# A one-layer decoder on one core: ten lower parts of the expert weights by VectorE, and another pace of splitting them

## The reference

```
x = layernorm(x + mixer(x))                 # state-space mixer, 4 sequences of 512
x = layernorm(x + xattn(x, ctx_1024))       # 16 heads of width 8, 256 keys
x = layernorm(x + ffn(x))                   # mixture of experts

def ffn(inputs):                            # E = 8 experts, top 2, D = 128, F = 512
    weights, selected = top_k(inputs @ gate_kernel, 2)
    weights = softmax(weights)
    # rows sorted by expert, each row once for each of its two experts
    hidden = silu(rows @ w0[e]) * (rows @ w1[e])
    rows_out = hidden @ wo[e]
    return weighted_sum_over_the_two(weights, rows_out)
```

## Time and profile before

| what | value |
|---|---|
| median of 3 runs | 422.5 us |
| the runs | 418.44, 422.5 and 1061.15 us |
| the profiled execution | 415.8 us |
| its span, first to last instruction | 414.5 us |
| granted TensorE clock, mean | 0.98 |
| busy: TensorE, VectorE, ScalarE, GpSimd | 349.5, 292.3, 235.2, 230.4 us |
| first and last product with a split weight on TensorE | start at 267.8 and 393.4 us |

### The profile page before, as it was taken

The page is one execution under the profiler, slowest core; times in us unless marked ns, Lnnn a source line. Parts: engine busy times, 40 slices in busy tenths (PEclk is TensorE's granted clock), DMA queues, the critical chain, the costliest instruction groups (busy, mean ns, idle before and its releaser), DMA issues.

```text
span 414.5 us, 9020 instructions
## 1 busy us (share of the span) xinstructions
PE 349.5 (84%) x2869; PEld 238.0 (57%) x2869; DVE 292.3 (71%) x836; ACT 235.2 (57%) x460; POOL 230.4 (56%) x341
## 2 busy tenths in 40 slices
PE   1999977888988999988878899988997999999900
PEld 1666645556544545444444445567776899898800
DVE  3555645888788888878796736376776877877737
ACT  2677644432667666455577687744644665666514
POOL 2660598855354435271569788546575445445525
PEclk9999999999999999999999999999999999999975
DMA  8933322636515040322624343211112211111054
GB/s 269 336 110 106 87 85 77 187 94 186 171 33 166 5 140 5 99 70 75 196 69 131 117 155 102 74 32 40 53 41 78 78 53 40 53 52 35 32 171 146
DMA packets 44461, 41.97 MB, mean 101 GB/s; under 512 B 4560, under 2 KB 38416, under 8 KB 44416
## 3 DMA queue, kind: packets, MB, share of 16 engines
q1 hardware_dynamic: 41136, 35.10, 28.1%
q0 software_dynamic: 2272, 4.69, 3.2%
q10 hardware_dynamic: 1008, 1.61, 1.1%
HBM read 26.36 MB, written 14.75 MB: 99 GB/s over the span
## 4 chain that ended last, share of the span: by engine, by line
PE 56%; DVE 20%; issue 7%; POOL 7%; ACT 4%; another core or an unknown queue 3%; DMA 2%; ACTq 0%; DVEq 0%; POOLq 0%
PE banks L1017 12%; DVE nm L1210 8%; PE banks L1044 6%; PE banks L1032 4%; PE banks L859 4%; PE banks L698 4%; PE banks L907 3%; PE banks L1045 2%; PE banks L755 2%; PE banks L937 2%; PE banks L763 2%; DVE ctx_in L1152 2%; PE banks L806 2%; PE banks L934 1%
## 5 line engine op out<-in xcount | busy, mean ns | idle before, releaser
L1210 DVE TENSOR_REDUCE nm<-banks 128x4 f32<-128x1024 f32 x64 | 78.1, 1220 | 17.5 <-PE banks L850 11.4
L1520 ACT ACTIVATE probs_all<-banks 128x1024 f32<-128x1024 f32 x64 | 65.4, 1023 | 36.0 <-PE banks L859 29.6
L1017 PE MATMUL banks<-w_split,scores_in 128*128 x234 | 64.5, 410 | 0.0
L1342 DVE TENSOR_TENSOR ctx_in<-ctx_in,banks 128x512 f32<-128x512 f32 x39 | 26.8, 687 | 27.3 <-ACT ctx_in L1567 21.4
L1017 PEld LDWEIGHTS banks<-w_split,scores_in 128*128 128x128 f32 x234 | 40.8, 189 | 7.7 <-issue 0.9
L1705 POOL DMA_INDIRECT slots_dram<-rows,place_u x32 | 31.9, 996 | 23.5 <-DVE count L1302 16.1
L1727 POOL DMA_INDIRECT y_dram<-x,scatter_u x39 | 38.5, 987 | 11.4 <-POOL x L1723 9.7
L1567 ACT ACTIVATE ctx_in<-banks 128x512 f32<-128x512 f32 x39 | 23.3, 599 | 36.7 <-PE banks L1017 31.9
L859 PE MATMUL banks<-scores_in 32*128 32x256 f32 x256 | 32.2, 326 | 12.0 <-ACT probs_all L1520 6.0
L1044 PE MATMUL banks<-w_split,scores_in 128*128 x156 | 39.1, 327 | 2.8 <-ACT scores_in L1573 2.1
L907 PE MATMUL banks<-probs_all,vals 128*9 128x256 f32 x512 | 39.7, 381 | 0.2
(11 more groups left out here) (230 smaller groups left out, 802.2 us busy)
## 6 DMA issues: line engine op xcount, KB each, us to landing
scores_in<-k_dram SPq DMA_DIRECT2D x32, 128.0 KB, 2.7
scores_in<-q_dram SPq DMA_DIRECT2D x32, 128.0 KB, 2.7
ctx_in<-in_L_ffn_w SPq DMA_DIRECT2D x16, 256.0 KB, 2.7
cs_wide<-cs_dram SPq DMA_DIRECT2D x14, 256.0 KB, 3.7
scores_in<-slots_dram SPq DMA_DIRECT2D x39, 65.0 KB, 1.9
k_dram<-split_qk SPq DMA_DIRECT2D x8, 256.0 KB, 2.5
q_dram<-split_qk SPq DMA_DIRECT2D x8, 256.0 KB, 2.3
ctx_in<-in_L_ffn_wo SPq DMA_DIRECT2D x8, 256.0 KB, 2.9
```

The source lines that it names most:

```text
L1017: m = TE.matmul(up_bank(i, j), xT[:, i % XT, xh, :], all_weights[:, c + j * FF:][:, bass.ds(expert_at[i], FF)], start=n == 0, stop=n == 2)
L1210: V.tensor_reduce(most, maxima_of(n).rearrange("p (j k q) -> p j k q", j=2, k=TPS), AX_X, ALU.max, negate=True).then_inc(s["nmax"], 1)
L1520: C.activation(probs(n).rearrange("p j k q -> p (j k q)"), EXPS, ACT.Exp, scale=SCALE).then_inc(s["probs"], 1)
```

## The change

Ten of the 24 subtractions, those of pieces 14 to 23, go from GpSimd to VectorE, with a semaphore of their own, w_lo_v. Pieces 0 to 3 are loaded at step 34 and the first is split at step 36; no piece is split at steps 40, 41 and 49. So pieces 0 to 3 are split at steps 36 to 39, 4 to 10 at steps 42 to 48, and 11 to 23 at steps 50 to 62, VectorE's ten at steps 53 to 62. The step of piece n loads piece n + 3 in place of n + 2. VectorE's subtraction stands in its queue where split_weights stands in the common list, and waits for ScalarE's copy of the same piece. SyncE's later loads and the first product of the experts wait for both semaphores. In turn_mixed a wait of GpSimd for its own instruction uses the common semaphore of that kind; the instructions are the same.

```diff
@@ -57,6 +57,7 @@
 W_HEAD, W_REST, W_OUT, W_ALL = 0, 2 * FF, 4 * FF, 6 * FF
 W_RING = NT * D // FF
 PIECES = 3 * NE
+POOL_PIECES = 14
 XG, AHEAD = 8, 4
 LAST_ADDED = SLOT_TILES - 3
 XT, TURNED_AHEAD, DOWN_LAG, HS = 3, 2, 3, 3
@@ -206,6 +207,7 @@
 CLEAR_FROM = 23
 TURNED_ALONE = max(END_HALVES) // 2 | 1
 LAST_MIXER = tile_step(NT - 1) + LAGS[0][1]
+WEIGHTS_FROM, WEIGHTS_OMITTED = LAST_MIXER + 2, (40, 41, 49)
 
 
 def front_order():
@@ -288,13 +290,13 @@
                 yield "evacuate", weighed // GR, 0
         yield from (stage for stage in after_attention(n) if stage[0] not in READY)
         yield from mixer_step(n)
-        if n == LAST_MIXER + 4:
+        if n == WEIGHTS_FROM:
             for i in range(W_RING):
                 yield "load_weights", i
-        elif n >= LAST_MIXER + 6 and piece < PIECES:
+        elif n >= WEIGHTS_FROM + 2 and n not in WEIGHTS_OMITTED and piece < PIECES:
             yield "split_weights", piece
-            if W_RING <= piece + 2 < PIECES:
-                yield "load_weights", piece + 2
+            if W_RING <= piece + 3 < PIECES:
+                yield "load_weights", piece + 3
             piece += 1
         yield from tiles_step(n)
         if UNREAD_FROM <= n < 4 and n != 2 or n >= ALL_MAXIMA - 1:
...
@@ -552,6 +554,15 @@
 
             return a["ctx_g0" if g == END_LAST else f"rows{g}"]
 
+        def split_parts(n):
+
+            e, i = divmod(n, 3)
+            raw = w_raw[:, n % W_RING, :]
+            if i < 2:
+                return raw, *(w_split[:, e, c + i * FF:c + (i + 1) * FF] for c in (W_HEAD, W_REST))
+            parts = w_split[:, e, W_OUT:].rearrange("p (c h d) -> p c h d", c=FC, h=2)
+            return raw.rearrange("p (c d) -> p c d", c=FC), parts[:, :, 0, :], parts[:, :, 1, :]
+
         def all_scattered(q):
             for r in range(Y_RING):
                 q.wait_ge(a[f"y_out{r}"], 16 * len(range(r, SLOT_TILES, Y_RING)))
@@ -653,7 +664,8 @@
                 q.wait_ge(s["q_mm"], B)
                 q.wait_ge(a["qw0"], 32 * B // 2)
                 q.wait_ge(a["qw1"], 32 * B // 2)
-                q.wait_ge(s["w_lo"], n - W_RING + 1)
+                q.wait_ge(s["w_lo"], min(n - W_RING + 1, POOL_PIECES))
+                q.wait_ge(s["w_lo_v"], n - W_RING + 1 - POOL_PIECES)
                 if i < 2:
                     SY.dma_start(w_raw[:, r, :], A[f"L0_ffn_w{i}"][e]).then_inc(a[f"e{r}"], 16)
                 else:
...
@@ -1009,7 +1021,8 @@
                 q.wait_ge(s["xT_hi"], i + 1)
                 q.wait_ge(s["xT_lo"], i + 1)
                 q.wait_ge(s["hid"], i - 1)
-                q.wait_ge(s["w_lo"], PIECES)
+                q.wait_ge(s["w_lo"], POOL_PIECES)
+                q.wait_ge(s["w_lo_v"], PIECES - POOL_PIECES)
                 if i == 1:
                     q.wait_ge(s["probs"], NPAIR)
                 for n, (xh, c) in enumerate(((0, W_HEAD), (0, W_REST), (1, W_HEAD))):
...
@@ -1301,6 +1314,13 @@
                 own.settle()
                 V.tensor_tensor(count[:, :], count[:, :], total, ALU.add).then_inc(s["counted"], 1)
 
+            def split_weights(n):
+                if n < POOL_PIECES:
+                    return
+                raw, head, rest = split_parts(n)
+                q.wait_ge(s["w_hi"], n + 1)
+                V.tensor_tensor(rest, raw, head.bitcast(F32), ALU.subtract).then_inc(s["w_lo_v"], 1)
+
             def count_tiles(part):
                 q.wait_ge(s["counted"], PART_BATCHES[part])
                 if part == LAST_PART:
...
@@ -1542,13 +1562,7 @@
                              ACT.Identity).then_inc(s["rows_x2"], 1)
 
             def split_weights(n):
-                e, i = divmod(n, 3)
-                raw = w_raw[:, n % W_RING, :]
-                if i < 2:
-                    head = w_split[:, e, W_HEAD + i * FF:W_HEAD + (i + 1) * FF]
-                else:
-                    raw = raw.rearrange("p (c d) -> p c d", c=FC)
-                    head = w_split[:, e, W_OUT:].rearrange("p (c h d) -> p c h d", c=FC, h=2)[:, :, 0, :]
+                raw, head, _ = split_parts(n)
                 q.wait_ge(a[f"e{n % W_RING}"], 16 * (n // W_RING + 1))
                 C.activation(head, raw, ACT.Identity).then_inc(s["w_hi"], 1)
 
...
@@ -1654,8 +1668,8 @@
             def turn_mixed(b):
                 bb = b % 2
                 q.wait_ge(s["sq"], TPS * (b + 1))
-                G.tensor_scalar(ss[:, bb, :], ss[:, bb, :], 1.0, DI * 1e-6, ALU.mult, ALU.add).then_inc(s["rms_in"], 1)
-                q.wait_ge(s["rms_in"], b + 1)
+                own.step(G.tensor_scalar(ss[:, bb, :], ss[:, bb, :], 1.0, DI * 1e-6, ALU.mult, ALU.add))
+                own.settle()
                 q.wait_ge(s["r1"], TPS * (b - 1))
                 G.tensor_tensor(rms[:, bb, :], ss[:, bb, :], minus_half[:, 0:TPS], ALU.pow).then_inc(s["rms"], 1)
 
...
@@ -1706,13 +1720,9 @@
                                          rows[:, b % 2, i // TPS, i % TPS, :], None).then_inc(a[f"slots{b % 2}"], 16)
 
             def split_weights(n):
-                e, i = divmod(n, 3)
-                raw = w_raw[:, n % W_RING, :]
-                if i < 2:
-                    head, rest = (w_split[:, e, c + i * FF:c + (i + 1) * FF] for c in (W_HEAD, W_REST))
-                else:
-                    raw = raw.rearrange("p (c d) -> p c d", c=FC)
-                    head, rest = (w_split[:, e, W_OUT:].rearrange("p (c h d) -> p c h d", c=FC, h=2)[:, :, h, :] for h in range(2))
+                if n >= POOL_PIECES:
+                    return
+                raw, head, rest = split_parts(n)
                 q.wait_ge(s["w_hi"], n + 1)
                 G.tensor_tensor(rest, raw, head.bitcast(F32), ALU.subtract).then_inc(s["w_lo"], 1)
```

More of the change, by code:

```diff
@@ L324 @@
     "bc_t bcT score_mm score diff fall xdt skip xdec decay mat state_mm state off_mm "
-    "y_mm y_sum y_gated sq yT_t yT rms_in rms out_mm r1 ln1_var ln1_in ln1 x1 x1_t x1T "
+    "y_mm y_sum y_gated sq yT_t yT rms out_mm r1 ln1_var ln1_in ln1 x1 x1_t x1T "
     "q_mm max_mm nmax nm_split nm_t nm_out exp_mm probs av_mm av_lo av_hi heads_t o_norm o_t oT wo_mm "
-    "r2 ln2_var ln2_in ln2 x2 x2_t x2T rows_x2 gate_mm logit ge topped chosen rank_mm counted w_hi w_lo "
+    "r2 ln2_var ln2_in ln2 x2 x2_t x2T rows_x2 gate_mm logit ge topped chosen rank_mm counted w_hi w_lo w_lo_v "
     "xg_t xT_hi xT_lo up_mm sil hid turn_mm hsT_hi hsT_lo down_mm y_half y_add y_x2 y_last "
@@ L1378, in vector_program @@
                           divide=divide, out_project=out_project, x2_norm=x2_norm, gate_top=gate_top, choose=choose,
-                          rank_chosen=rank_chosen, count_tiles=count_tiles,
+                          rank_chosen=rank_chosen, split_weights=split_weights, count_tiles=count_tiles,
                           rank_tiles=rank_tiles, place_tiles=place_tiles,
```

## The result

| | kernel before | changed kernel |
|---|---|---|
| median of 20 executions | 419.72 us | 422.50 us |
| lowest | 416.44 us | 420.73 us |
| profiled execution | 415.8 us | 422.87 us |
| its span | 414.5 us | 421.5 us |
| granted TensorE clock, mean | 0.98 | 0.966 |

The ratio is 1.0073, 95% interval 1.0053 to 1.0092: about 3 us slower. It leaves out executions more than 1.5% above the fastest of the same kernel, which of the changed kernel are 6 of 20, at 429 to 432 us with a mean clock of 0.93 to 0.946. The profiled execution of the kernel before, at 415.8 us, is faster than all of the twenty that were timed, so the two traces lie 7 us apart and the medians 2.8.

What follows compares the result with a forecast made beforehand. Bound: the chain through all engines up to step 50, TensorE's own queue from step 52. Terms +0.5 + 0 + 0 + 0.8 = +1.3 us on 418.4 gave 419.7, rounded to 420; range 414 to 426 us.

Steps and rivals of the forecast that it cites:

- part 2: Steps 40, 41 and 49 without a split: claimed 0, range 0 to -1.0 us; maxima's split 2.5 us earlier.
- The starting point: Base of the sum: the lower undisturbed run, 418.4 us, chosen over the stated median of 422.5 us.
- The copy at step 37: ScalarE's new copy at step 37, where there is no gap, delays exponential 38 on the chain: +0.5 us.
- No split at 40, 41 and 49: Exponentials 42 and 50 start 0.52 us earlier, but 43 and 51 wait for the fourth indirect write: 0.
- The rule read from a few rows: A batch's first steps can't go on before its fourth indirect write ends; TensorE's signals arrive 0.75 to 0.8 us after.
- Loads further ahead: Loads one piece earlier: ScalarE's 0.42 us landing wait goes, the value-bank copy holds exponential 46; 0, range 0 to -0.3.
- The subtraction on VectorE: Ten subtractions at steps 53 to 62: 0.68 us each, range 0.68 to 1.54; only their place costs.
- The late count: Step 57: tile count waits behind VectorE's subtraction, ends at 255.5, delaying the placing of tiles: +0.8 us.
- Rival B: Tile count's whole 2.7 us delay reaches TensorE, or subtractions take 1.54 us: +3.2 us, 421.6 us; chance 0.15.
- The rule that the two engines exclude each other: Two-input VectorE work and GpSimd's SBUF reads block each other; from step 53 VectorE loses blockers, GpSimd's roots gain some.
- Rival D: TensorE stands still 1.5 us at 254, clock falls, expert stage loses tens of us: over 440 us; chance 0.02.

Runs made afterwards that it cites:

- Run 6: The changed kernel with no split at step 37 and one at step 40; ratio 1.0013 to the kernel before.
- run 7: The changed kernel, split at 40 not 37, choices summed by one-input reduction, tile count ahead of its step's subtraction; ratio 1.0008 to the kernel before.
- run 11: Changed kernel, split at 40 not 37, one-input reduction, count ahead of subtraction, indirect writes spread over four steps; ratio 0.9893 to kernel before, median 415.89 us.
- run 9: The kernel before with the four indirect writes of batches 0 to 4 spread, one in each of four steps; ratio 1.0007 to the kernel before.
- run 8: The kernel before with ten subtractions on VectorE and the tile count ahead of its step's subtraction, old pace; ratio 0.9984 to the kernel before.
- run 12: The changed kernel, split at 40 not 37, one-input reduction, tile count still behind the subtraction; ratio 1.0004 to the kernel before, median 426.74 us.
- run 1: The changed kernel with all 24 subtractions on GpSimd, so the new pace alone; ratio 1.0040 to the kernel before.
- run 3: The changed kernel with the tile count moved ahead of its step's subtraction on VectorE; ratio 1.0033 to the kernel before.
- run 4: The changed kernel with four filler matmuls on TensorE ahead of its wait for the late tile count; ratio 1.0054 to the kernel before.
- run 10: The kernel before with ten subtractions on VectorE, count ahead of its step's subtraction, and indirect writes spread over four steps; ratio 0.9950 to the kernel before.
- run 2: The kernel before with ten subtractions moved to VectorE, old pace kept; ratio 1.0018 to the kernel before, profiled execution 428.17 us.
- run 5: The changed kernel with VectorE's two-input sum of choices replaced by a one-input reduction; ratio 1.0259 to the kernel before.

## Why the prediction was wrong

The forecast number, 420.0, lay under the 422.5 shown as the time before, and the kernel became slower. The sum of the steps said +1.3 us, and +3.1 (0.73% of 419.7) were measured. Two steps failed. The base on which the sum was put turned "slower" into a number that says "faster" (item 1). And part 2 put at nothing what the new pace does to VectorE's choosing at step 43, which cost 1.2 us (item 7). The sign of the sum was right, and the 422.5 us measured lie in the range of 414 to 426, which is wide enough for either sign.

1. *The starting point.* "I set the forecast on the lower" of two runs: twenty executions later the median before is 419.7, so 418.4 was too low by 1.3 us. More important, a forecast of "slower by 1.3" written as a number below the stated median says "faster". Who doubts a base should add to the base that is stated.

2. *The copy at step 37*: +0.5 forecast, +0.47 in the trace. Right. Run 6 removes it.

3. *No split at 40, 41 and 49*: 0 forecast, "timed by the count". Right in runs 6 and 7, where exponential 42 is half a microsecond earlier and 43 isn't; shown from the other side by run 11, where the writes no longer hold and 0.85 us of the two half microseconds stays. The rule read from a few rows, that the steps can't go on before the fourth indirect write ends, held under test (run 9) in that the stop goes with the burst; its mechanism stays open.

4. *Loads further ahead*: 0 forecast, with exponential 46 held where it is; exponential 45 gained 0.2 us and 46 lost it. Right.

5. *The subtraction on VectorE*: 0.68 us each forecast, 0.688 in the median. Right, and the move itself has no cost that run 8 can tell.

6. *The late count*: +0.8 forecast. In runs 6 and 12, at full clock, exponentials 59 and 60 together are 0.65 us later. Right within 0.2 us. Rival B's price, +3.2 us, meets the measured +3.1 by luck: it took the count's whole delay of 2.7 us or subtractions of 1.54 us, and neither came.

7. *The step that failed: part 2, and the use of the rule.* Part 2 counted what GpSimd has to do behind the indirect writes and not what of VectorE stands beside it. The rule that the two engines exclude each other was there, but applied only "from step 53 on", where engines changed. The cost came at step 43, where no instruction changed engines. Part 2 saw that the split of the maxima comes 2.5 us earlier and stopped there: in the kernel before that short work stood beside VectorE's sum, and a subtraction began 0.25 us behind it; in the changed one a subtraction gets ahead of the sum by 0.08 us. The sum itself grew by 1.06 us, and exponential 46 came 1.24 us later against 45, the largest term apart from the clock. It is there again in runs 1, 3 and 4, and on the first comparison in 9 and 10 (2.05 and 2.03 us long) and, by 0.4 us, in 6, 7 and 12. The comparisons beside the sum gave the bound, with 176 ns in the median and 1992 at most; I should have asked for every such instruction of VectorE whether a GpSimd subtraction would now stand beside it.

8. *Rival D, the clock, had 0.02 and an absurd price.* I wrote that a gap of 1.5 us is nothing new and that a low clock would last through the expert stage. In fact the clock fell within 2 us of the end of the gap in the profiled execution and came back after 6.8 us; in run 2 after 20.5; in runs 5, 6 and 12 it didn't fall there. Steps 59 to 61 cost 3.6 us in the changed kernel's trace, of which 0.65 is the wait. At a mean clock of 0.973 the one execution that the changed kernel has took 421.2 us, the 22 of the one before 417.7 to 420.6 with a median of 418.6, so the greater part of the 3 us isn't the clock. That part is items 2, 4, 6 and 7: 0.5 - 0.2 + 0.65 + 1.2 = 2.15 us. With the three places mended 2.7 us of the 3.1 are gone (run 7).

Left open: the microsecond in the expert stage of the profiled execution; why all six executions of run 5 had a mean clock of 0.958 or less; what brings the low clock at 227 to 233 in runs 1, 7, 8 and 9; and what holds TensorE's results at the end of a burst of indirect writes.

## What to carry to other kernels

When work moves in time, list the instructions of VectorE with two inputs in SBUF on the chain, and look at what GpSimd reads beside them now and then; another form with one input (a reduction in place of a sum) took the sum out of this lottery, though not the comparisons beside it. On an in-order queue the price of an added instruction is that of its wait, and it is paid by the first urgent stage behind it (here VectorE waited 1.78 us ahead of 0.69 us of work, and 0.65 us of it reached the chain): put the subtraction behind the count. A gap of TensorE should be priced twice, once as waiting and once as the chance that the clock falls after it. And a forecast in microseconds belongs on the base that is stated for the kernel before.

## What the runs showed of the hardware

- In five groups of steps the exponential behind four indirect writes from GpSimd (1.26 us apart from the second on) started 0.7 to 1.2 us after the end of the fourth, and 1.3 to 2.3 us after the modelled end of its scores on TensorE; with the writes spread it started 0.05 us after its scores, 1.3 to 2.2 us sooner against the one ahead of it. Not all results of TensorE were held: ScalarE took one at 214.86, behind the first write of a burst that ran from 213.71 to 218.61.
- A gap of 1.47 us in TensorE's work, in a stretch in which it was otherwise busy, stands in five profiled executions; 6.8 and 20.5 us at the lower clock followed in two of them, none in three. Of the executions with the new pace, 20 of 50 had a mean clock of 0.95 or lower with the gap, 5 of 48 without it.
- The low stretches in these traces were 3.4, 6.8, 10.2, 13.7 or 20.5 us long, ahead of the last 22 us of the kernels; one of 10.2 us, in runs 3 and 5, lay ahead of every changed instruction.
- A VectorE sum of 128x16 with two inputs in SBUF took 1.23 us when a GpSimd subtraction of 1.27 us had started 0.08 us earlier, and 0.17 us when GpSimd's 128x32 work began with it; the reduction with one input took 0.19 us beside one. The Trainium skill, "SBUF — State Buffer", section "Who interferes with whom", has it that a VectorE instruction with two SBUF inputs contends with a GpSimd instruction that reads SBUF; these rows agree.
- VectorE did the 128x512 subtraction in 0.69 us, GpSimd in 1.27.
